# Flamingo cross-attention layers on one core: the second attention's keys and queries for four heads at a time, split into even and odd halves and handed on by DMA

## What is computed

```
q = (q_in @ Wq + bq).reshape(b, sq, N_HEADS, D_Q).transpose(0, 2, 1, 3)      # 16 heads of 64
k = (k_in @ Wk + bk).reshape(b, sk, N_HEADS, D_Q).transpose(0, 2, 1, 3)
q = _rope(q)
k = _rope(k)
scores = jnp.einsum('bhqd,bhkd->bhqk', q, k) * (1.0 / np.sqrt(D_Q))
scores = jnp.where(valid[:, None, None, :], scores, -jnp.inf)
attn = jax.nn.softmax(scores, axis=-1)
out = jnp.einsum('bhqk,bhkd->bhqd', attn, v)
```

## Time and profile before

| | |
|---|---|
| median of 3 runs | 2907.51 us (2904.9 to 2911.35) |
| the profiled execution | 2903.99 us |
| its span, first to last instruction | 2901.8 us |
| mean granted TensorE clock | 0.949 |
| TensorE busy | 2618.3 us (90%), 32664 matmul rows |
| VectorE busy | 2005.0 us (69%) |
| ScalarE busy | 1448.7 us (50%) |
| GpSimd busy | 1387.3 us (48%) |

### The profile page before, as it was taken

One profiled execution on the slowest core, in us unless ns is written; L12 is line 12 of the kernel. 1 busy time (PEld: TensorE's weight loads), 2 busy tenths in 40 slices (PEclk: granted clock), 3 DMA queues, 4 the chain that ended last, 5 costly groups with the idle time before them and its releaser, 6 DMA issues. The chain is left out here.

```text
span 2901.8 us, 82200 instructions
## 1 busy us (share of the span) xinstructions
PE 2618.3 (90%) x32664; PEld 1564.2 (54%) x32664; DVE 2005.0 (69%) x6348; ACT 1448.7 (50%) x2248; POOL 1387.3 (48%) x1227
## 2 busy tenths in 40 slices
PE   4679999999988659999999999999999999996598
PEld 3433333333345636666666666666666666664365
DVE  3468888888865667776766767767677667662655
ACT  2247777777755035545446445455464454443122
POOL 2000000000001037887888878878888788885100
PEclk8689999999998869999999999999999999997799
DMA  5521111111100020000000000000000000001000
GB/s 151 152 90 22 26 23 25 22 26 23 25 24 8 22 80 7 19 13 7 19 13 6 18 13 8 24 7 19 13 7 19 13 7 8 7 2 52 0 0 14
DMA packets 109630, 75.20 MB, mean 26 GB/s; under 512 B 43907, under 2 KB 101579, under 8 KB 108752
## 3 DMA queue, kind: packets, MB, share of 16 engines
q1 hardware_dynamic: 109264, 70.08, 8.7%
HBM read 56.61 MB, written 13.43 MB: 24 GB/s over the span
## 5 line engine op out<-in xcount | busy, mean ns | idle before, releaser
L1508 ACT ACTIVATE a_probs<-psS 128x1024 f32<-128x1024 f32 (+1 forms) x448 | 431.4, 963 | 609.8 <-PE psS L1389 606.4
L645 ACT ACTIVATE a_probs<-psS 128x1024 f32<-128x1024 f32 (+2 forms) x512 | 443.2, 866 | 207.7 <-PE psS L586 207.3
L1825 POOL TENSOR_TENSOR a_acc<-a_acc,a_probs 128x512 f32<-128x512 f32 x320 | 407.0, 1272 | 193.4 <-ACT a_probs L1508 183.8
L1412 PE MATMUL psX<-a_probs,a_values 128*64 128x256 f32 x3328 | 443.4, 384 | 0.0
L672 DVE CUSTOM_DVE_ANT_0 a_junk<-psT,a_mask 128x384 f16<-128x384 f32 (+1 forms) x683 | 378.1, 573 | 61.5 <-PE psT L562 41.6
L1827 POOL TENSOR_TENSOR a_acc<-a_acc,a_probs 128x512 f32<-128x512 f32 x320 | 407.0, 1272 | 25.1
L1669 DVE CUSTOM_DVE_ANT_0 a_junk<-psT,a_mask 128x400 f16<-128x400 f32 (+1 forms) x513 | 281.9, 572 | 139.0 <-PE psS L1364 74.1
L1669 DVE CUSTOM_DVE_ANT_0 a_junk<-psS,a_mask 128x400 f16<-128x400 f32 (+1 forms) x511 | 281.2, 572 | 133.5 <-PE psT L1364 73.4
L989 POOL MEMSET r_ones<- 128x128 f16 x1 | 0.2, 205 | 695.2 <-POOLq L719 695.2
L1412 PEld LDWEIGHTS psX<-a_probs,a_values 128*64 128x64 f32 x3328 | 223.6, 137 | 103.4 <-issue 28.8
L1799 POOL TENSOR_TENSOR a_klo<-a_kt,a_khi 128x400 f16<-128x400 f32 (+1 forms) x256 | 242.6, 948 | 18.9 <-ACT a_khi L1560 18.9
(11 more groups left out here) (342 smaller groups left out, 5605.9 us busy)
## 6 DMA issues: line engine op xcount, KB each, us to landing
a_kd<-p_kst SPq DMA_DIRECT2D x24, 416.0 KB, 3.1
a_wq<-in_wq SPq DMA_DIRECT2D x64, 128.0 KB, 2.1
a_keys<-a_kd SPq DMA_DIRECT2D x96, 75.0 KB
p_ctx<-in_ctx SPq DMA_DIRECT2D x8, 768.0 KB
a_ctx<-in_ctx SPq DMA_DIRECT2D x8, 768.0 KB
a_queries<-a_lowest SPq DMA_DIRECT2D x256, 0.5 KB, 2.0
p_mask_raw<-in_mask_t SPq DMA_DIRECT2D x16, 224.0 KB, 4.4
a_queries<-a_qd SPq DMA_DIRECT2D x64, 52.0 KB
```

What stands on the lines that cost most here:

```text
L645: nc.scalar.activation(dst, src, ACT.Exp).then_inc(exp_done, 1)
L1412: ins = nc.tensor.matmul(w.sums[n % 2][64 * hd:64 * hd + 64, 0:T], w.values[:, n % 2, c, 64 * hd:64 * hd + 64], w.probs[:, k % RING1, 2 * ...
L1508: nc.scalar.activation(dst, src, ACT.Exp).then_inc(exp_done, 1)
L1825: nc.gpsimd.tensor_tensor(acc, acc, src[:, :, 0, :], ALU.add).then_inc(sum_step, 1)
```

## The change

Keys and queries are made for four heads (two pairs, a "quad") at once. The columns of `Wk` and `Wq` are reordered, so that one piece holds the even dimensions of four heads (4 times 32 = 128 output partitions) and the other the odd ones. Each piece is three products of 128 output columns, in the 128*128 form. The second set of weights (`wk1x`) is gone. VectorE's rotation of a quarter is six instructions for four heads where it was three for two (`rotate`), and its rotation of a query six where it was two and a sum on GpSimd (`rotate_query`).

The rotated halves no longer stand where the scores want them (a head's 64 dimensions on 64 partitions). ScalarE and GpSimd write them into a staging buffer (`w.made`), and SyncE moves them by 8 transfers a pair (`give_first`, `give_last`, four each) into `w.both`, which the scores and the ahead products read. A new wait holds ScalarE's `key_hi` and `query_hi` until the transfers of the quad before have landed.

The loop starts one iteration earlier (-4). Slots are cut into halves: the weighted values come first in the second half, and the pieces are dealt out anew (`UNITS1`, `VALUES1`, `KEY_TIMES1`). The ring has five banks; the output sums have one bank for every pair instead of two in turn, and ScalarE copies them out (`take_out`) instead of the spread inverses, which become a piece of the ring.

```diff
-AHEAD1 = [2, 2, 1, 1, 1, 1, 0]
...
-VALUES1 = {2: (0, 1), 4: (2, 3)}
-ITERATIONS1 = range(-3, PAIRS1 + 1)
+QUADS1 = PAIRS1 // 2
+HALVES1 = [(sl, half) for sl in range(SLOTS1) for half in range(2)]
+UNITS1 = {(1, 1): 0, (2, 0): 1, (2, 1): 2, (3, 0): 3, (4, 1): 4, (5, 0): 5, (5, 1): 6, (6, 0): 7}
+VALUES1 = {(1, 0): 0, (3, 0): 1, (4, 0): 2, (6, 1): 3}
+KEY_TIMES1 = {(0, 0): 0, (3, 1): 1}
+NEAR1 = 5
...
+def split_in(it, sl):
+
+    return it % 2 * 2 + (0 if sl == 2 else 1) if sl in (2, 5) and quad_in(it) is not None else None
...
+        w.near = [m.psS[:, 2 * BANK:3 * BANK], m.psS[:, 3 * BANK:4 * BANK], m.psT[0][:, :], m.psT[1][:, :], m.psT[2]]
+        w.sums = m.psO[:, 0:T]
...
+            def blocks(n):
+                for hd in range(2):
+                    for part in range(2):
+                        p0, r0 = 32 * (2 * (n % 2) + hd), 64 * hd + 32 * part
+                        yield slice(p0, p0 + 32), slice(r0, r0 + 32), part
+
+            def give_first(n):
+                sp.wait_ge(q_lo, n // 2 + 1)
+                sp.wait_ge(k_lo, 4 * (n // 2) + 2)
+                width = T + 2 * QUARTER[0]
+                for src, dst, part in blocks(n):
+                    sp.dma_start(w.both[dst, n % KEPT1, :, 0:width], w.made[0][src, :, part, :]
+                                 ).then_inc(keys_in[n % KEPT1][0], 16)
...
-            sp.dma_start(raw(1), dram["wk1x"]).then_inc(w_loaded, 16)
...
+                    if sl == 0 and is_pair(it + 3):
+                        if it >= 1:
+                            sp.wait_ge(b_full, SLOTS1 * it)
+                        give_first(it + 3)
+                        if it % 2 == 0:
+                            give_last(it + 3)
+                    if it % 2 == 1 and sl == 5 and is_pair(it + 3):
+                        give_last(it + 3)
...
-                    for hd in range(2):
-                        c0 = p * P + 64 * hd
-                        ins = nc.tensor.matmul(out[64 * hd:64 * hd + 64, 0:width], w.wk[:, part, split, c0:c0 + 64], moving,
-                                               start=(i == 0), stop=(i == 2), skip_group_check=True)
+                    ins = nc.tensor.matmul(out[:, 0:width], w.wk[:, split, c0:c0 + P], moving, start=(i == 0), stop=(i == 2))
...
-                pe.wait_ge(k_hi, 4 * n + j + 1)
-                pe.wait_ge(q_hi, n + 1)
+                wait_given(pe, n, j)
...
+            def key_hi(q, j):
+                for part in range(2):
+                    act.wait_ge(near_free[bank_of(("key", q, j, part))], uses_of(("key", q, j, part)))
+                if q > 0:
+                    wait_given(act, 2 * q - 2, j)
+                    wait_given(act, 2 * q - 1, j)
+                made, o = made_at(j)
+                width = QUARTER[j]
+                nc.scalar.copy(made[:, 0, :, o:o + width], w.kt[:, j % 2, :, 0:width]).then_inc(k_hi, 1)
...
+                nc.vector.scalar_tensor_tensor(w.swung[:, 0, 0:width], even, bias[:, 0:1], w.sin[:, cols], ALU.add, ALU.mult)
+                nc.vector.scalar_tensor_tensor(even, even, bias[:, 0:1], w.cos[:, cols], ALU.add, ALU.mult)
+                nc.vector.scalar_tensor_tensor(w.swung[:, 1, 0:width], odd, bias[:, 1:2], w.sin[:, cols],
+                                               ALU.add, ALU.mult).then_inc(k_step, 1)
+                dve.wait_ge(k_step, 2 * done + 1)
+                nc.vector.tensor_tensor(w.kt[:, j % 2, 0, 0:width], even, w.swung[:, 1, 0:width],
+                                        ALU.subtract).then_inc(near_free[bank_of(names[0])], 1)
+                nc.vector.scalar_tensor_tensor(odd, odd, bias[:, 1:2], w.cos[:, cols], ALU.add, ALU.mult).then_inc(k_step, 1)
+                dve.wait_ge(k_step, 2 * done + 2)
+                nc.vector.tensor_tensor(w.kt[:, j % 2, 1, 0:width], odd, w.swung[:, 0, 0:width],
+                                        ALU.add).then_inc(near_free[bank_of(names[1])], 1)
```

More of the change, by code:

```diff
@@ L1126, in count_pieces @@
     for it in ITERATIONS1:
[L1127 to L1130, removed]
+        for sl, half in HALVES1:
+            if is_pair(it + 2) and (sl, half) in UNITS1:
+                order += [("ahead", it + 2, UNITS1[sl, half], hd) for hd in range(2)]
+            if turned_in(it) is not None and 2 <= sl <= 5 and half == 1:
                 order.append(("turn", turned_in(it), sl - 2))
[L1132 to L1138, removed]
+            if is_pair(it + 1) and (sl, half) in VALUES1:
+                order.append(("value", it + 1, VALUES1[sl, half]))
+            if query_in(it) is not None and (sl, half) == (6, 1):
+                order.append(("query", query_in(it)))
+            if quarter_in(it, sl, half) is not None:
+                order += [("key", quad_in(it), quarter_in(it, sl, half), part) for part in range(2)]
+            if is_pair(it + 1) and (sl, half) == (2, 1):
                 order.append(("max", it + 1))
-            if is_pair(it - 1) and sl == 3:
+            if is_pair(it - 1) and (sl, half) == (3, 0):
                 order.append(("sums", it - 1))
-            if leaves_in(it) is not None and sl >= 5:
+            if is_pair(it - 1) and (sl, half) == (4, 1):
+                order.append(("spread", it - 1))
+            if leaves_in(it) is not None and sl >= 5 and half == 1:
                 order.append(("project" if sl == 5 else "leave", leaves_in(it)))
@@ L1273, in _ @@
             load_masks(1)
-            for n in range(2):
-                load_queries(n)
+            for q in range(2):
+                load_queries(q)
             for it in ITERATIONS1:
@@ L1476, in _ @@
                         for part in range(2):
-                            key(it + 3, sl - 3, part)
-                    if is_pair(it + 1) and sl == 2:
+                            key(quad_in(it), quarter_in(it, sl, half), part)
+                    if is_pair(it + 1) and (sl, half) == (2, 1):
                         turn_max(it + 1)
-                    if sl == 0 and is_pair(it - 1):
-                        weigh(it - 1, SLOTS1 - 1)
-                    if sl > 0 and is_pair(it):
-                        weigh(it, sl - 1)
@@ L1585, in _ @@
             take_x(1)
-            act.wait_ge(w_loaded, 48)
-            for i in range(3):
+            act.wait_ge(w_loaded, 32)
+            for i in range(2):
                 nc.scalar.copy(weights(i)[0], raw(i)).then_inc(w_hi, 1)
@@ L1783, in weights_lo @@
             def weights_lo():
-                pool.wait_ge(w_hi, 3)
-                for i in range(3):
+                pool.wait_ge(w_hi, 2)
+                for i in range(2):
                     hi, lo = weights(i)
```

402 lines of the change are left out of this document (207 added, 195 removed).

## The result

The changed kernel takes 2859.49 us (median of 4 runs, 2854.07 to 2866.76), the kernel before beside it 2906.20 us: a ratio of 0.9841, with a 95% interval of 0.982 to 0.9862. It is faster, as forecast, but by 47 us where 122 were forecast, and 2859 lies above the range of 2735 to 2845.

The account below looks back on a forecast made before the run. TensorE was taken to set the pace. The terms -129 - 28.5 + 48 - 11 - 8 + 5 = -123.5 us took 2903.99 to 2780.5; with 3.5 us for the median, 2784 us, range 2735 to 2845.

Parts of the forecast that it names:

- the paragraph on the transfers: Hand-over through SyncE's queue to the ahead products and `key_hi`: cover of 0.5 to 1.6 us, costed at nothing.
- The late hand-over: Rival: GpSimd falls behind, TensorE waits before the third ahead product every second pair; 51 us, 2835 us; chance 0.20.
- Held ScalarE: Rival: transfers land one after another, `key_hi` holds slot 3's exponential, scores 8 us late; 240 us, 3024 us; chance 0.05.
- A free change of form: Rival: switching TensorE between product forms costs nothing here; 48 us less, 2736 us; chance 0.15.
- the product at half pace: Rival: full 128*128 key products take 2.1 us a quarter, so the saving on keys is gone; 2909 us; chance 0.05.
- Keys, -129: TensorE's key quarters in the loop: 1.04 us each as before, but serving four heads; 129 us less.
- Changes of form, +48: TensorE in plain pairs: 24 switches of product form instead of 16, 0.10 us each over 60 pairs; 48 us more.
- Queries, -28.5: TensorE's query products: 0.92 us a quad instead of a pair, 31 times; 28.5 us less.
- Projection, -11: A batch's first pair: TensorE's 1.61 us wait behind VectorE's division goes, 7 times; 11 us less, 0 at the other end.
- Third pair, -8: A batch's third pair: half of 2.52 us of waits for rotation and exponential goes, 7 times; 8 us less, between 0 and 18.
- Start, +5: Ahead of the first pair: more VectorE rotation before the first exponential; 5 us more, between 2 less and 10 more.
- GpSimd's split of 800 elements: GpSimd's work on keys: two such splits cost at most four of 400, 2 times 1.90 us.

Follow-up runs that it names:

- Experiment 1: Against the changed kernel, the next batch's context load is issued behind the pair's hand-over transfers instead of ahead of them; 2824.49 us.
- experiment 2: Against the changed kernel, load order kept, but for batches 1 to 7 only 64 KB plus last rows of context loaded instead of 768 KB; 2834.91 us.
- Experiment 3: Against the changed kernel, the first key quarter of each batch's fifth pair is made in slot 1 instead of slot 0; 2831.65 us.
- experiment 7: Against the kernel with both lists put right, each slot's weighted values are cut in two around the half slot's other work; 2841.02 us.
- experiment 6: Against the kernel with both lists put right, every quarter of keys is computed twice into the same bank; 2917.33 us.
- both lists put right: Changed kernel with the context load behind the hand-over and the fifth pair's first key quarter in slot 1; 2804.63 us, 2805.71 us when run again.

## Why the prediction was wrong

**The step that failed** is the paragraph on the transfers, which puts nothing into the sum for the hand-over. It had `key_hi` wait for "8 issues and a landing, about 5.5 us after that split, some 8 us into the pair", with ScalarE there "at about the same time", so no wait. In the first pair of a batch the split ends at 1671.67 (start 1669.96, 1.71 us) and the cast starts at 1683.73: 12.1 us, by these rows:

| | forecast | measured |
|---|---|---|
| eight issues | 2.9 | 2.52 + 2.88 = 5.4 |
| other issues between them | 0 | 0.58 + 1.64 + 0.74 = 2.96 |
| landing of the last | 2.5 | 1683.73 - 1680.30 = 3.4 |
| gaps | 0 | 0.3 |

The issue was taken from four small transfers at 1.44 us and is 2.5 to 2.9 us a four. The work ahead of it in the queue was not looked at, though SyncE's list in the kernel has the load ahead of the hand-over. Experiment 1 shows its price, 35 us, and experiment 2 that most of it hangs on the size of that load.

**The step that was missing** is the due time. The sum took each pair for a plain one. The keys of a quad are now made from slot 0 of the pair in which they begin, and at the turn of a batch they wait for a context whose last piece GpSimd ends only in that same half slot. The kernel before made the next batch's keys from slot 3 of the sixth pair, more than a pair later. The forecast named no wait on the context. Experiment 3 shows its price: 28 us by the runs, 23 by the seven fifth pairs. In both places part of the price is the lower clock behind the stand, for which the forecast had no term either.

**The rivals.** The late hand-over foretold waits of the ahead products in every second pair; the waits of the loop have one such line, of 0.2 us, once. Held ScalarE is the mechanism that came, "the cast into the staging buffer waiting for such a DMA". It cost something in one pair of eight (in the seventh the cast waits some 3 us as well, and that is covered), and it came through another door: what TensorE missed was not the exponential but the bank behind the copy of the maxima. Six waits of 3 to 4 us came where the rival had thirty of 8. A free change of form fell by experiment 7, the product at half pace by experiment 6.

**Term by term.**
- Keys, -129: right. The quarter measures 1.03 to 1.04 us and a doubled one costs 112 us, with the shortfall in three places of the batch, put down above to waits and the clock.
- Changes of form, +48: right. 0.106 for 0.10.
- Queries, -28.5: the query of a quad takes 1.01 us (1797.65 to 1798.66) with a change of form behind it, where 0.92 was taken: nearly right, 3 us over 31 quads.
- Projection, -11: its wait is gone from the loop.
- Third pair, -8: inside its bounds of 0 and 18, partly by luck. It gained 2.89 us, 1.35 more than the plain pairs' mean of 1.54. But not half of the waits went in the batch of the earlier trace rows: the late rotation's 1.91 us are gone and the wait for the exponential grew from 0.61 to 2.69. The gain comes mostly from four batches in which that wait was 2.21 us before. It is the largest wait left:

```profile
1730.16 0.82 PE L1457 MATMUL psS<-a_both 64*128 64x256 f16 x6 [2.69 <-ACT a_probs L1576]
```
- Start, +5: 8.3, inside its bounds of -2 and 10. VectorE's quarter takes the 3.62 us of the sum (1046.75 to 1050.37), but a cast of ScalarE waits for the hand-over there too, with the next quarters behind it. The first exponential, which answers to the earlier trace rows, and that cast:

```profile
1074.84 0.86 ACT L1633 CAST xn<-a_kt 128x800 f16<-128x800 f32 x1 [10.58 <-DMA a_both<-xn]
...
1101.08 1.02 ACT L1576 ACTIVATE a_probs<-psS 128x1024 f32<-128x1024 f32 x1 [0.26 <-PE psS L1457]
```
- GpSimd's split of 800 elements takes 1.71 us, under the bound of 1.90.

**What is left.** With both lists put right the kernel takes 2805 us, 21 above the forecast and inside the range. Of that, 3 us are the start. The terms give (129 + 28.5 - 48)/62 = 1.77 us a pair. The second, sixth and eighth pairs of that kernel gained 1.34 to 1.38, the seventh 1.77; this is some 8 us over seven batches, of which the dearer change of form is a small part (8 times 0.006 a pair). The most, some 17 us, is in the fourth and fifth pairs, where the context is turned: together they gained 1.17 us (48.37 to 47.20) where two pairs were to gain 3.54. TensorE's waits in these two come to 1.4 us where they were 0.3 before; which work takes the remainder was not tried.

## What to carry to other kernels

A loop whose list repeats once in eight passes has to be costed once in each of the eight places, since the mean pair hid both waits. For every transfer that someone waits for, write down what stands ahead of it in its queue in that pass, bytes included; for every product moved earlier, when the last thing that it waits for is ready in the worst pass, and whether it needs all of it. A removed cost is read from the plain pass, a new one from the pass with the most in it.

## What the runs showed of the hardware

- A transfer of 32 partitions with two rows each, inside the core, holds SyncE's queue 0.6 to 0.7 us (2.52 to 2.88 for four in the batch shown, though up to 3.70 in experiment 1), where the four small ones of the earlier trace rows took 0.36 each. The size made no difference to see: 132 KB and 100 KB issue and land alike. From the page of the changed kernel, with KB each and the median from issue to landing:

```profile
a_both<-xn SPq DMA_DIRECT2D x256, 132.0 KB, 2.4
a_both<-a_made_late SPq DMA_DIRECT2D x256, 100.1 KB, 2.3
```

- Behind a stand of 3 us the granted clock was 0.57 for seven microseconds, and a quarter of keys took 2.09 us instead of 1.04. TensorE had worked 0.39 us of the 3 before:

```profile
1772.00:1775.00 3.00, 0.39 (x8) 0.10 (x3) 0.00 (x0) 1.02 (x1) 3.00 (x4) 0.85 0.01 2
```

  Without the wait (experiment 3) the same stretch has a clock of 1.00. A wait of TensorE can thus cost more than its length. It need not: of seven stands of 2.68 to 2.69 us in the third pairs (experiment 6), six were followed by work at the lower clock, which cost 1.5 us a pair, and one was not; in the kernel with the doubled keys none was.
- The waits also show in the mean clock: 0.935 in the changed kernel, 0.945 with both lists put right.
